# Weighed samples of a deformable convolution: the four corners of a value stored side by side and summed by one reduction

## The chip, the cores and the metric

The kernel runs on one core of a Trainium2 chip. The metric is the device time of one execution, in microseconds. Each TensorE matmul, VectorE operation, ScalarE activation and GpSimd gather below belongs to this one core; the engines run side by side and meet by semaphores.

## The reference

Four blocks follow one another on x of shape (4, 128, 32, 32): an attention with 32 reduced channels (L0), a bottleneck with a deformable convolution (L1), an attention with 16 query channels (L2) and a group norm with an attention of 128 channels (L3). The change lies in L1. What L1 computes:

```python
h = relu(bn(conv1x1(x, w1)))                 # 128 -> 32 channels
off = conv3x3(h, woff) + boff                # 27 channels: 9 taps of (y, x) and a mask
y, x_ = off[:, :18] + base positions         # one sampling place per tap and pixel
mask = sigmoid(off[:, 18:])
samp = (gather(y0, x0) * (wy0 * wx0) + gather(y0, x0 + 1) * (wy0 * wx1)
      + gather(y0 + 1, x0) * (wy1 * wx0) + gather(y0 + 1, x0 + 1) * (wy1 * wx1)) * mask
out = einsum('bckhw,ock->bohw', samp, w2) + b2
return relu(bn(conv1x1(relu(bn(out)), w3)) + x)
```

So each sampled value is a sum over four corners, each a gathered value times a weight: for each pixel 9 taps x 32 channels.

## The kernel before, in words

**Work and tiles.** A batch is one image of 1024 pixels, in 8 tiles of 128 pixels; a pixel is a partition. "(3,7)" is batch 3, tile 7. Everything is fp32 (P = 128, R = 32 channels, TAPS = 9, CORNERS = 4).

**The table.** Per batch the kernel builds a table in DRAM, one row per cell of 2 x 2 neighbouring pixels: 4 corners x 32 channels = 128 floats. `l1_rows` on VectorE (lines 1758 to 1769) works out the row of each tap, `l1_corners` (1774 to 1787) the four weights of each tap; its last four operations, at line 1787, write 72 results each, one corner each, into `corner_w`, where the four corners of a tap lie side by side, so that each of them stores every fourth float. Line 1783 does two products of the same size with results side by side.

**The gather.** GpSimd runs 4 x 8 x 9 = 288 indirect DMAs (line 323), one per batch, tile and tap; each brings one table row per pixel into `got[:, t, k, :]`, 128 floats (corner outermost, channel innermost). `got` has 8 slots, one per tile. Before tile t of the next batch it waits for `slot_free`, which the weighing increments.

**The weighing and the additions.** `l1_weigh` waits for the nine gathers of its tile and for `turn_w`, the 36 weights of the tile, which ScalarE copies into PSUM (line 1171) after its copy of the tile before. It multiplies 1152 gathered floats by their weights into `weighed` (line 1796), in the same layout (tap, corner, channel). `l1_add` adds corners 2 and 3 onto 0 and 1 (line 1807, 576 elements), drains, and adds the two remaining corners into `samples` (line 1809, 288 elements: tap, channel). `samples` has two buffers, freed by TensorE's transposes (`st_mm`).

**Behind it.** TensorE's `l1_turn` (line 488) transposes the samples of a tile, ScalarE copies them (`samplesT`), and when all 8 tiles of a batch are there `l1_conv2` (line 496) and `l1_conv3` (line 511) follow, then `l1_end` on VectorE (line 1819), and with it the batch's L2 and L3.

**The order of work.** Each engine has its instructions in one order written out by hand. L0 of batches 1 to 3, then L2 and L3 of the batches before, are interleaved with the tiles of L1: on VectorE `l1_weigh` and `l1_add` of a tile stand between the row maxima (line 1714 for L0 and L2, line 1897 for L3), the norms (1746, 1838, 1840), the residual additions (1753, 1846, 1914) and so on; on TensorE `l1_turn` stands between scores (360, 391, 625), transposes (635) and values (572, 647). Mostly the next block's operations stand between two tiles of L1. After tile (3,7) come the rest of L1 of batch 3, its L2 and its L3, with nothing gathered any more.

Of the kernel before, what the change touches and what calls it, by code (L numbers as in the profile page):

```python
# [7 lines left out]
P = 128  # L8
# [3 lines left out]
R = 32  # L12
QK2 = C // 8
TAPS = 9
CORNERS = 4
# [37 lines left out]
def build(nc, x_dram, weights_dram, out_dram):  # L53
    fp32, fp32r, bf16, int32 = mybir.dt.float32, mybir.dt.float32r, mybir.dt.bfloat16, mybir.dt.int32
    ALU, ACT, X = mybir.AluOpType, mybir.ActivationFunctionType, mybir.AxisListType.X
# [3 lines left out]
    with ctx:  # L59
        def sb(name, shape, dt=fp32):  # L60
            return ctx.enter_context(nc.sbuf_tensor(name, shape, dt))

        def sem(name):
            return ctx.enter_context(nc.semaphore(name))
# [50 lines left out]
        got = sb("got", [P, TILES, TAPS, CORNERS * R])  # L115
        weighed = sb("weighed", [P, TAPS, CORNERS * R])
        samples = sb("samples", [P, 2, TAPS * R])
# [65 lines left out]
        slot_free = sem("slot_free")  # L183
        sample_ready, st_mm, st_copied = sem("sample_ready"), sem("st_mm"), sem("st_copied")
# [72 lines left out]
        turn_w = d1[:, TURNS * P:TURNS * P + TAPS * CORNERS]  # L257
# [1449 lines left out]
        def _(dve):  # L1707
# [85 lines left out]
            def l1_weigh(b, t):  # L1793
                dve.wait_ge(got_sem[t], 16 * TAPS * (b + 1))
                dve.wait_ge(turn_w_ready, TILES * b + t + 1)
                nc.vector.tensor_tensor(weighed[:, :, :].rearrange("p k (c r) -> p (k c) r", r=R),  # L1796
                                        got[:, t, :, :].rearrange("p k (c r) -> p (k c) r", r=R),
                                        turn_w.rearrange("p (k a) -> p k a", a=1)
                                        .to_broadcast([P, TAPS * CORNERS, R]), ALU.mult).then_inc(slot_free, 1)
                dve.drain()  # L1800
                if t == TILES - 1:
                    dve.sem_inc(table_free, 1)

            def l1_add(b, t):
                if TILES * b + t >= 2:
                    dve.wait_ge(st_mm, TILES * b + t - 1)
                nc.vector.tensor_tensor(weighed[:, :, 0:2 * R], weighed[:, :, 0:2 * R], weighed[:, :, 2 * R:4 * R], ALU.add)
                dve.drain()
                nc.vector.tensor_tensor(samples[:, t % 2, :].rearrange("p (k r) -> p k r", r=R), weighed[:, :, 0:R],
                                        weighed[:, :, R:2 * R], ALU.add).then_inc(sample_ready, 1)  # L1810
                dve.drain()

            def l1_samples(b, t):
                l1_weigh(b, t)
                l1_add(b, t)
# [160 lines left out]
            for n in range(4, 8):  # L1976
                l0_max(2, n)
            shift_parts(1, shift0_ready)
            l1_weigh(0, 0)
            l1_add(0, 0)  # L1980
            l1_weigh(0, 1)
            l1_add(0, 1)
            l0_norm(1, 0)
            l0_q(3, 0)
# [357 lines left out]
```

## Time and profile before

| what | value |
|---|---|
| median of 3 runs | 548.77 us (544.84 to 549.81) |
| the profiled execution, its own time | 544.07 us |
| its span | 542.3 us |
| granted TensorE clock, mean | 0.953 |
| TensorE busy | 485.2 us, 89% |
| VectorE busy | 316.7 us, 58% |
| ScalarE busy | 289.7 us, 53% |
| GpSimd busy | 277.5 us, 51% |

The span is the part of the execution that the trace covers; 1.8 us of the execution's time lie outside it. Shares are averages over the span. TensorE's matmuls are pipelined, so that its busy share is not its share of peak. A row of the trace names an engine, a line of the kernel, and the tiles written and read (`weighed<-got,pd` writes `weighed` from `got` and a PSUM tile); in brackets stands how long the engine was idle before it, and what ended this.

### The profile page before, as it was taken

To read this page: it belongs to the slowest core of one execution; us is meant where nothing else is said; L and a number is where in the kernel's file an instruction comes from. 1 tells how busy PE (TensorE), PEld (TensorE's weight loads), DVE (VectorE), ACT (ScalarE), POOL (GpSimd) and SP (SyncE) were. 2 spreads that over 40 slices of the span, in tenths; PEclk is the share of its full clock that TensorE was granted. 3 is DMA by queue.
4 is the path that set the end of the run, shared out by engine and by line. 5 is a ranking of instruction groups with operands and counts; after the bars stand their busy time and mean duration, and the time that the engine had idled before them with its cause. 6 is when DMAs were issued, how large, how long until landed. Compare 5 with 4: busy or idle time off the path is not lost.

```text
span 542.3 us, 7578 instructions
## 1 busy us (share of the span) xinstructions
PE 485.2 (89%) x2756; PEld 328.3 (61%) x2756; DVE 316.7 (58%) x560; ACT 289.7 (53%) x517; POOL 277.5 (51%) x292
## 2 busy tenths in 40 slices
PE   6897899787889799899988899998989899898997
PEld 4434464434534369557766847685956667594776
DVE  4746454657557676775387675478476567125322
ACT  5366632773576475247565436675525565532553
POOL 0000177777777777777777777777777500000000
PEclk9998759989999689999999999999899999799999
DMA  6000111113122111113113111113111100100001
GB/s 230 0 1 1 49 54 52 52 53 97 50 68 81 51 54 55 48 54 99 54 51 93 51 52 54 53 51 93 54 54 48 45 1 1 39 1 1 1 1 39
DMA packets 12708, 26.94 MB, mean 50 GB/s; under 512 B 4992, under 2 KB 5888, under 8 KB 12672
## 3 DMA queue, kind: packets, MB, share of 16 engines
q0 software_dynamic: 9216, 18.89, 11.7%
q1 hardware_dynamic: 3024, 6.52, 3.2%
q10 hardware_dynamic: 432, 1.05, 0.5%
q8 instruction: 22, 0.36, 0.3%
q14 instruction: 14, 0.11, 0.1%
HBM read 21.99 MB, written 4.46 MB: 49 GB/s over the span
## 4 chain that ended last, share of the span: by engine, by line
POOL 51%; PE 23%; issue 17%; DVE 3%; ACT 3%; DMA 2%; DVEq 1%; POOLq 0%; ACTq 0%
POOL got L323 51%; PE pd L647 4%; PE pq L391 2%; PE pq L635 2%; DVE neg_max L1714 2%; PE pc L416 1%; PE pc L625 1%; PE pa L625 1%; PE pa L572 1%; ACT cells L1221 1%; DMA xall<-x_dram 1%; PE pa L360 1%; PE pc L572 1%; PE pa L340 1%; PE pc L360 1%
## 5 line engine op out<-in xcount | busy, mean ns | idle before, releaser
L323 POOL DMA_INDIRECT got<-cell_table,rows_all x288 | 277.3, 963 | 152.5 <-issue 87.5
L1714 DVE TENSOR_REDUCE neg_max<-pa 128x1 f32<-128x1024 f32 x48 | 58.7, 1223 | 34.8 <-PE pa L360 34.3
L647 PEld LDWEIGHTS pd<-v3T,probsT 128*128 128x128 f32 x512 | 60.5, 192 | 7.0 <-ACT probsT L1171 3.6
L647 PE MATMUL pd<-v3T,probsT 128*128 128x128 f32 x512 | 63.0, 277 | 1.0 <-ACT probsT L1171 0.7
L391 PE MATMUL pq<-q_stack,k_stack 128*128 128x512 f32 x120 | 55.4, 511 | 7.8 <-ACT expT L1205 4.6
L1796 DVE TENSOR_TENSOR weighed<-got,pd 128x1152 f32<-128x1152 f32 x32 | 43.2, 1349 | 24.5 <-ACT pd L1171 15.7
L360 PE MATMUL pa<-k_stack,q_stack 96*128 96x512 f32 x96 | 40.7, 512 | 9.2 <-DVE neg_max L1714 9.2
L1205 ACT ACTIVATE expT<-pq 128x512 f32<-128x512 f32 x64 | 35.6, 595 | 21.9 <-PE pq L391 21.0
L1171 ACT ACTIVATE probsT<-pq 128x1024 f32<-128x1024 f32 (+1 forms) x32 | 32.3, 1008 | 24.8 <-PE pq L635 18.0
L391 PEld LDWEIGHTS pq<-q_stack,k_stack 128*128 128x128 f32 x120 | 24.5, 216 | 31.4 <-ACT expT L1205 14.1
L1309 ACT ACTIVATE expT<-pq 128x512 f32<-128x512 f32 x56 | 31.1, 595 | 12.3 <-PE pq L391 11.6
L635 PEld LDWEIGHTS pq<-wts,probs 128*128 128x128 f32 x256 | 29.2, 141 | 9.2 <-issue 6.0
L360 PEld LDWEIGHTS pa<-k_stack,q_stack 96*128 96x128 f32 x96 | 18.9, 230 | 25.2 <-DVE neg_max L1714 20.2
L416 PE MATMUL pc<-expT,vT 128*64 128x512 f32 x128 | 33.9, 648 | 0.1
L635 PE MATMUL pq<-wts,probs 128*128 128x128 f32 x256 | 33.4, 274 | 0.6 <-ACT probs L1339 0.5
L1171 ACT ACTIVATE samplesT<-pd 96x384 f32<-96x384 f32 x32 | 15.4, 482 | 34.3 <-PE pd L488 34.2
L1221 ACT ACTIVATE cells<-pd,bn_t,bn_s 32x512 f32<-32x512 f32 x32 | 24.6, 770 | 13.5 <-PE pd L449 12.9
L1897 DVE TENSOR_REDUCE neg_max<-pa 128x1 f32<-128x1024 f32 x16 | 19.5, 1222 | 20.8 <-PE pa L625 20.7
L625 PE MATMUL pc<-k,q_offs 128*128 128x512 f32 x64 | 30.3, 596 | 0.0
L625 PE MATMUL pa<-k,q_offs 128*128 128x512 f32 x64 | 30.2, 595 | 0.0
L1897 DVE TENSOR_REDUCE neg_max<-pc 128x1 f32<-128x1024 f32 x16 | 19.5, 1220 | 15.2 <-PE pc L625 15.2
L572 PE MATMUL pa<-vT,expT 128*128 128x129 f32 x192 | 25.7, 291 | 0.9 <-ACT expT L1309 0.9
(180 smaller groups left out, 792.0 us busy)
## 6 DMA issues: line engine op xcount, KB each, us to landing
got<-cell_table,rows_all POOLq DMA_INDIRECT x288, 2.4
cell_table<-tabS SPq DMA_DIRECT2D x4, 512.0 KB, 2.9
out_dram<-cells SPq DMA_DIRECT2D x7, 256.0 KB, 2.1
xall<-x_dram SPq DMA_DIRECT2D x2, 512.0 KB, 8.4
wts<-weights_dram SPq DMA_DIRECT2D x1, 778.5 KB, 5.9
xall<-x_dram ACTq DMA_DIRECT2D x2, 256.0 KB, 5.0
xall<-x_dram ACTq DMA_DIRECT2D x1, 512.0 KB, 8.2
cell_table<-tabS SPq DMA_DIRECT2D x4, 64.0 KB, 2.8
```

The lines of the kernel that those rows point to most:

```text
L323: nc.gpsimd.indirect_dma_start(got[:, t, k, :], None, tables[b % 2], bass.IndirectOffsetOnAxis(ap=rows_all[:, b, at:at + 1], axis=0)).then ...
L360: last = nc.tensor.matmul(pair[:, half(h)], q_stack[stack][0:3 * R, tile(t)], k_stack[stack][0:3 * R, half(h)], start=True, stop=True)
L391: nc.tensor.matmul(bank, k_stack[stack][:, tile(j)], q_stack[stack][:, half(h)], start=True, stop=True)\
L416: last = nc.tensor.matmul(o0_bank(b, h)[2 * R * n:2 * R * (n + 1), :], vT0[:, j, :], expT[:, j, half(h)], start=g == 0, stop=g == TILES // ...
L572: last = nc.tensor.matmul(o2_bank(t), expT[:, j, tile(t)], vT[:, j, :], start=j == 0, stop=j == TILES - 1)
L625: last = nc.tensor.matmul(pair[:, half(h)], q3[:, tile(t)], k3[:, half(h)], start=True, stop=True)
L635: last = nc.tensor.transpose(pq[:, tile(j)], probs[:, t % 2, tile(j)], ident)
L647: last = nc.tensor.matmul(d0[:, 0:C], probsT[:, tile(j)], v3T[:, j, :], start=j == 0, stop=j == TILES - 1)
L1171: return nc.scalar.activation(to, bank, ACT.Copy)
L1714: nc.vector.tensor_reduce(neg_max[:, t:t + 1], pair[:, :], axis=X, op=ALU.max, negate=True)\
L1796: nc.vector.tensor_tensor(weighed[:, :, :].rearrange("p k (c r) -> p (k c) r", r=R), got[:, t, :, :].rearrange("p k (c r) -> p (k c) r", r=R),
L1897: nc.vector.tensor_reduce(neg_max3[:, t:t + 1], (pa, pc)[t % 2][:, :], axis=X, op=ALU.max, negate=True)\
```

## The change

The weighing stores its products in another order: tap, channel, corner, with the corner innermost, so that consecutive results of the instruction (channel by channel) are 4 floats apart. What it reads, and in which order, is as before. The two additions and the drain between them are replaced by one `tensor_reduce` over the innermost 4 floats, which reads 1152 contiguous floats and writes the 288 of `samples`. Waits and semaphores stay where they are.

```diff
 def l1_weigh(b, t):
     dve.wait_ge(got_sem[t], 16 * TAPS * (b + 1))
     dve.wait_ge(turn_w_ready, TILES * b + t + 1)
-    nc.vector.tensor_tensor(weighed[:, :, :].rearrange("p k (c r) -> p (k c) r", r=R),
-                            got[:, t, :, :].rearrange("p k (c r) -> p (k c) r", r=R),
-                            turn_w.rearrange("p (k a) -> p k a", a=1)
-                            .to_broadcast([P, TAPS * CORNERS, R]), ALU.mult).then_inc(slot_free, 1)
+
+    nc.vector.tensor_tensor(weighed[:, :, :].rearrange("p k (r c) -> p k c r", c=CORNERS),
+                            got[:, t, :, :].rearrange("p k (c r) -> p k c r", r=R),
+                            turn_w.rearrange("p (k c a) -> p k c a", c=CORNERS, a=1)
+                            .to_broadcast([P, TAPS, CORNERS, R]), ALU.mult).then_inc(slot_free, 1)
     dve.drain()
...
 def l1_add(b, t):
     if TILES * b + t >= 2:
         dve.wait_ge(st_mm, TILES * b + t - 1)
-    nc.vector.tensor_tensor(weighed[:, :, 0:2 * R], weighed[:, :, 0:2 * R], weighed[:, :, 2 * R:4 * R], ALU.add)
-    dve.drain()
-    nc.vector.tensor_tensor(samples[:, t % 2, :].rearrange("p (k r) -> p k r", r=R), weighed[:, :, 0:R],
-                            weighed[:, :, R:2 * R], ALU.add).then_inc(sample_ready, 1)
+    nc.vector.tensor_reduce(samples[:, t % 2, :], weighed[:, :, :].rearrange("p k (r c) -> p (k r) c", c=CORNERS),
+                            axis=X, op=ALU.add).then_inc(sample_ready, 1)
     dve.drain()
```

## Rows read from the trace of the kernel before

**Rows 1.** The page: TensorE's busy share, the chain by engine, the gathers' group.

```profile
PE 485.2 (89%) x2756; PEld 328.3 (61%) x2756; DVE 316.7 (58%) x560; ACT 289.7 (53%) x517; POOL 277.5 (51%) x292
...
POOL 51%; PE 23%; issue 17%; DVE 3%; ACT 3%; DMA 2%; DVEq 1%; POOLq 0%; ACTq 0%
...
L323 POOL DMA_INDIRECT got<-cell_table,rows_all x288 | 277.3, 963 | 152.5 <-issue 87.5
```

**Rows 2.** The chain in order of time, 425 to 445 us: start, length, what.

```profile
431.79 1.35 DVE weighed L1796
...
433.28 0.76 DVE weighed L1807
...
434.11 0.47 DVE samples L1809
```

**Rows 3.** Busy time (instructions) in two stages of the gathers' part.

```profile
249.60:340.50 90.90, 85.38 (x555) 63.86 (x554) 58.61 (x96) 49.44 (x90) 68.99 (x72) 1.00 0.21 65
340.50:431.80 91.30, 86.33 (x552) 64.77 (x549) 57.27 (x94) 49.99 (x90) 68.45 (x71) 0.98 0.19 58
```

The columns: the stretch, its length, busy us of PE, PEld (weight loads), DVE, ACT and POOL, then granted clock, DMA share and GB/s.

**Rows 4.** Who waited for whom, 65 to 432 us: total us, times, longest.

```profile
DVE weighed L1796 <- DMA got<-cell_table,rows_all: 8.7, 3, 4.7
...
PE pa L360 <- DVE neg_max L1714: 7.1, 7, 1.3
```

**Rows 5.** Timeline at tiles (2,7) and (3,7), VectorE and TensorE.

```profile
340.48 1.35 DVE L1796 TENSOR_TENSOR weighed<-got,pd 128x1152 f32<-128x1152 f32 x1 [3.85 <-DMA got<-cell_table,rows_all]
...
343.31 0.53 PE L488 MATMUL pd<-wts,samples 128*96 128x128 f32 x3 [0.58 <-DVE samples L1809]
...
434.62 0.53 PE L488 MATMUL pd<-wts,samples 128*96 128x128 f32 x3 [2.36 <-DVE samples L1809]
```

**Rows 6.** Timeline: slot 3 weighed in batch 1, its first gather in batch 2.

```profile
218.06 1.34 DVE L1796 TENSOR_TENSOR weighed<-got,pd 128x1152 f32<-128x1152 f32 x1
...
281.84 0.95 POOL L323 DMA_INDIRECT got<-cell_table,rows_all  x1 [0.30 <-issue]
```

**Rows 7.** VectorE's groups by line and shape: busy us, mean ns, idle before.

```profile
L1714 DVE TENSOR_REDUCE neg_max<-pa 128x1 f32<-128x1024 f32 x48 | 58.7, 1223 | 34.8 <-PE pa L360 34.3
...
L1807 DVE TENSOR_TENSOR weighed<-weighed 128x576 f32<-128x576 f32 x32 | 24.2, 757 | 2.7
...
L1809 DVE TENSOR_TENSOR samples<-weighed 128x288 f32<-128x288 f32 x32 | 14.8, 461 | 2.4
L1892 DVE TENSOR_SCALAR q_offs<-pc,bq3s 128x512 f32<-128x512 f32 x8 | 5.9, 751 | 4.1 <-PE pc L608 3.8
...
L1887 DVE TENSOR_SCALAR h<-x,gscale,gbias 128x512 f32<-128x512 f32 x8 | 4.0, 546 | 0.3
```

**Rows 8.** Lines 1787 and 1783: duration ns min/median/max, first and last start.

```profile
L1787 DVE TENSOR_TENSOR corner_w<-wy,probsT x16: 279/290/310, 74.1 to 210.5; 128x72 f32<-128x72 f32 x16
```

```profile
L1783 DVE TENSOR_TENSOR wy<-probsT x8: 219/231/302, 73.7 to 209.8; 128x72 f32<-128x72 f32 x8
```

**Rows 9.** Timeline: the four operations of line 1787 in batch 0, merged.

```profile
74.15 0.72 DVE L1787 TENSOR_TENSOR corner_w<-wy,probsT 128x72 f32<-128x72 f32 x4
```

**Rows 10.** Timeline, 354 to 432 us: TensorE and VectorE behind tiles (3,0) to (3,6).

```profile
359.69 1.41 DVE L1709 SCALAR_TENSOR_TENSOR k_stack<-pa,wts,k_stack 32x512 fp32r<-32x512 f32 x2 [1.25 <-ACT k_stack L1278]
```

```profile
379.33 0.84 PE L488 MATMUL pd<-wts,samples 128*96 128x128 f32 x3
...
398.71 0.66 PE L581 MATMUL pq<-wts,oT 128*128 128x128 f32 x4 [0.72 <-DVE oT L1840]
...
420.97 0.49 PE L488 MATMUL pd<-wts,samples 128*96 128x128 f32 x3
```

**Rows 11.** Timeline, 408 to 411 us: a gather beside the additions of tile (3,4).

```profile
408.46 0.75 DVE L1807 TENSOR_TENSOR weighed<-weighed 128x576 f32<-128x576 f32 x1
408.53 1.50 POOL L323 DMA_INDIRECT got<-cell_table,rows_all  x1 [0.30 <-issue]
...
409.29 0.46 DVE L1809 TENSOR_TENSOR samples<-weighed 128x288 f32<-128x288 f32 x1
```

## The prediction

> **What bounds the kernel now.** The page first: its busy shares, then its chain of waits [rows 1]. TensorE (PE) is busy for 89% of the span, and yet half of the chain that ended last is GpSimd's gathers. Then the chain in order of time around the last gather [rows 2]: up to there nearly every piece is a gather, with 0.30 us of issue between two; at 431.79 the last has landed, and tile (3,7) (batch 3, tile 7) goes through the weighing and both additions to TensorE's transposes and second convolution. From there the chain is TensorE work until 542.3. So the kernel has two parts: up to 431.8 us a stream of 288 gathers sets a floor, and TensorE and VectorE run beside it in an order written by hand; after that TensorE alone counts, and none of the changed code runs.
>
> How tight is each in the first part? The windows by stage [rows 3]: TensorE is busy for 85.4 and 86.3 us of two stages of 91 us, VectorE for 58. TensorE is nearly the bound itself. The waits [rows 4]: the 32 weighings waited for a gather three times only, 8.7 us together, at most 4.7, which is (3,7)'s; 3.85 is (2,7)'s [rows 5]. TensorE's own waits behind these two were 0.58 and 2.36 us [rows 5]. These 2.9 us are all the room that TensorE has before a delay of its stream reaches the end, and also all that it could win if the gathers came sooner.
>
> Could a slower weighing hold up the gathers? A slot is refilled 8 tiles later. The closest case of the 24 is slot 3 of batch 1: weighed from 218.06, filled anew from 281.84 [rows 6], over 62 us later. That cover can't be used up by any price below.
>
> **The change, part by part.**
>
> *The two additions* take 757 and 461 ns [rows 7], and with the 0.07 us between them (from start to start 0.83 [rows 2]) 1.29 us. In their place stands one reduction of 1152 elements to 288 from SBUF, which the trace doesn't show. Nearest rows [rows 7]: the reductions of 1024 elements from PSUM take 1.22 us, 1.19 ns per element, which is 1.37 for 1152; the weighing has 1152 elements and takes 1.35 [rows 2]. From above: if each of the 288 results cost an element's time more (the two additions differ by 288 elements and 296 ns), 0.30 more, 1.65. From below: a one-input operation of 512 elements takes 0.55 us from SBUF and 0.75 from PSUM; if the reduction ran at that better pace, about 1.35 x 0.55/0.75 = 1.0. I take 1.35, the row of its own kind, so +0.06 us a tile (from -0.3 to +0.36).
>
> *The weighing* keeps its operands, its 1152 products and its reading order. Only the store changes: neighbouring results now lie four floats, 16 bytes, apart. The nearest row is the corner weights at line 1787, which store 72 results exactly so, against the products at line 1783, 72 results stored side by side from the same kinds of operands: medians of 290 and 231 ns [rows 8], 59 ns more. A gain is excluded, since the reading is as before. Bounds: nothing, if the 59 ns is a fixed cost or belongs to the operands (+0.06 at most); proportional, 0.82 ns per result, x 1152 = +0.94 us; and one whole element time per result with a little of it hidden in a short instruction, 1152 x 1.03 = +1.19. Against a full price stands that the four at line 1787 follow each other quickly: 0.72 us for all, one alone 0.29, so 0.143 from start to start [rows 9], 2.0 ns per result, which just leaves room for a doubled store and proves none. I take the middle of the two prices, +1.07: the weighing takes about 2.42 us.
>
> The Trainium skill, page "SBUF — State Buffer", in its remark on cachelines (section "Door 1: The DMA port swizzle"), says that SBUF is served in lines of 16 bytes and that an access stream which goes to a new line each time pays a penalty. That speaks against exactly this store, and it agrees with the longer row at line 1787; the page prices no VectorE store, so the sum goes by the rows.
>
> *Sum per tile*: 1.07 + 0.06 = +1.13 us on VectorE, 36 us over 32 tiles, on an engine that is idle for over a third of either stage [rows 3]. What of it reaches TensorE? I followed the seven tiles (3,0) to (3,6) in the timeline, four of whose turning points stand in [rows 10]. (3,0): idle of 0.47 and 1.25 before the next two results that TensorE needs takes it all. (3,1): its samples were ready at 378.79, TensorE took them at 379.33: 0.54 of room, 0.59 passes on. (3,2): idle of 1.04, 1.66 and 2.22 follows: nothing. (3,3): VectorE is busy without a gap until the result that TensorE waits for at 398.71: all 1.13. (3,4): 1.26 idle right behind: nothing. (3,5): ready at 420.66, taken at 420.97: 0.82 passes on. (3,6): ready at 425.75, taken at 427.39: nothing. Together 2.54 of 7.9, a share of 0.32.
>
> The terms: 31 tiles before the last x 1.13 x 0.32 = 11.2 us of delay of TensorE's stream; less the 2.9 us that it waits anyway at (2,7) and (3,7); then the last tile, which lies on the chain with nothing beside it [rows 2]: +1.13. **+9.4 us.** The rest, from 436 on, only moves. The profiled execution took 544.07 us (span 542.3 and 1.8 around it), so 553.5 for its like. The median of the runs shown is 4.7 us above it; carried over, the forecast is 558.2 us.
>
> *What the change gives back.* The gathers of 0.94 us are sometimes longer: their mean is 963 ns [rows 1] against a median of 944, of which by far the most of them are within a few ns, 288 x 19 ns = 5.5 us in all. Of the 25 that took over 0.97 us, 22 overlap one of the two additions, and end just after it; one is shown, 1.50 us long, behind an addition that began just before it [rows 11]. Beside weighings and the reductions for maxima lie many gathers of 0.94.  So the additions, with two inputs in SBUF, hold GpSimd up, and both go. The stream would end some 5.3 us earlier. In my sum that is worth nothing, as TensorE and VectorE arrive later than the last gather anyhow; it counts in the first rival.
>
> The Trainium skill says as much, in the same page's section "Who interferes with whom": an instruction of VectorE with two SBUF inputs is in GpSimd's way when that reads SBUF, one with a single SBUF input isn't. The trace agrees (22 of 25).
>
> **The rivals.**
>
> *A, the store costs nothing.* For it: the pace of the four at line 1787 [rows 9], and the chance that the 59 ns is a fixed cost. Then the tile costs +0.06 and the gathers end 5.3 us earlier. TensorE can use 2.9 of that, since it is ready for (3,7)'s transposes 2.36 us before the samples, and 0.58 more is won at (2,7). The +0.06 of each tile costs 31 x 0.06 x 0.32 = 0.6, and 0.06 once more: -2.9 + 0.7 = -2.2: 541.9, or 546.6 by the median. Faster than before, though less than 1%. The point at which the sign turns: x(31 x 0.32 + 1) = 2.9, x = 0.27 us per tile.
>
> *B, the price is there but mostly covered.* If the earlier tiles pass on a tenth: 3.5 - 2.9 + 1.13 = +1.7, 545.8 or 550.5. For it: VectorE has over a third of its time free [rows 3]. Against: TensorE already waits behind VectorE in this part, for maxima seven times [rows 4].
>
> *C, VectorE becomes the bound in stretches.* With 1.25 us per tile and a share of 0.6: 23.3 - 2.9 + 1.25 = +21.6, 565.7 or 570.4. For it: each existing wait of TensorE behind VectorE, as that for the maxima [rows 4], grows one for one, and most lie in the early batches, where I did not follow the tiles. Against: the seven tiles that I followed.
>
> *D, the reduction runs faster than I think* (1.0 us) and the store costs nothing: then -0.3 a tile and TensorE's waits behind VectorE shrink: -2.9 - 0.3 - 31 x 0.3 x 0.32 = -6.2, 537.9 or 542.6. It needs both unknowns at their low ends.
>
> **How the numbers follow.** About 1%, 5.5 us, is what a measurement of this kernel tells from no change. Forecast 0.52, A 0.20, B 0.12, C 0.11, D 0.05. Slower by over 1%: nine tenths of the forecast's and all of C's, 0.58. Within 1%: the rest of the forecast, B, and most of A, 0.35. Faster by over 1%: D and a little of A, 0.07. Likeliest case alone: with 1.0 to 1.55 us per tile (both prices at their highest) the same sum gives +8.0 to +14.0, 557 to 563. The whole range takes in A below, and most of C above: 544 to 568.
>
> **What the profile after would show.** The weighing at about 2.4 us (A: 1.35; between 2.3 and 2.55 the price is as bounded). One reduction per tile at 1.35. VectorE's busy time up by some 35 us to 352. Gathers without long ones, mean 0.945, last one landing at 426 to 427. No weighing of (3,7) waiting for its gather; the chain before 440 on TensorE and VectorE and no longer on GpSimd. After the last weighing as before, TensorE's 110 us. I am wrong if the weighing stays under 1.6 us, or if it is at 2.4 and the start of (3,7) has moved by less than 3 us.

## The result and the profile after

The changed kernel takes 567.1 us (median of 4 executions, 563.3 to 568.8) against 546.8 before (4 executions, 544.5 to 549.8): a ratio of 1.036, 95% interval 1.027 to 1.044, slower by some 20 us. The direction of the prediction holds. The time lies inside its range, by 0.9 us, and only because the range was drawn wide enough to take in most of rival C; the forecast's own figure, +9.4 us, is half of what came. The ratios below leave out executions that lay well above the fastest of their kernel, most of all two of the four of `reduce_only` and seven of the twelve of `mix_23`.

The profiled execution took 565.97 us, its span is 564.2. The page of the changed kernel, in the order of the page: busy shares, the granted TensorE clock in 40 slices, the chain by engine.

```profile
PE 496.9 (88%) x2756; PEld 333.4 (59%) x2756; DVE 349.3 (62%) x528; ACT 290.2 (51%) x517; POOL 272.3 (48%) x292
...
PEclk9998759789879868999999999999899999889999
...
PE 60%; DVE 21%; DVEq 7%; ACT 7%; issue 3%; DMA 1%; ACTq 0%
```

Three things stand here. VectorE's busy time rose by 32.6 us. The same 2756 matmuls are busy for 11.7 us longer than in [rows 1], at a lower mean clock (0.936 against 0.953), so about half of the 21.9 us by which the span grew is longer matmuls, the other half more idle time. That holds against this one execution of before; a fairer partner comes further down. And GpSimd is gone from the chain that ended last, where it was 51%: the gathers bound nothing any more.

The new instructions by line (duration in ns, least, median, greatest; first and last start in us), then the gathers, all of the changed kernel:

```profile
L1797 DVE TENSOR_TENSOR weighed<-got,pd x32: 2199/2266/2432, 91.2 to 452.9; 128x1152 f32<-128x1152 f32 x32
```

```profile
L1808 DVE TENSOR_REDUCE samples<-weighed x32: 1334/1353/1354, 93.6 to 455.3; 128x288 f32<-128x1152 f32 x32
```

```profile
L323 POOL DMA_INDIRECT got<-cell_table,rows_all x288: 940/945/1079, 67.5 to 426.1; - x144
```

The weighing went from 1.35 to 2.27 us: 0.918 us more for 1152 results, 0.80 ns each. The reduction takes 1.351, as forecast. From the start of the weighing to the end of the samples a tile took 2.738 us (median of 32) and takes 3.725: +0.987. And the gathers lost their long ones: the greatest was 1.5 us [rows 11], now it is 1.08; their last starts 3.3 us earlier, although the first starts 2.0 later.

At tile (3,7), VectorE and TensorE of the changed kernel:

```profile
452.89 2.29 DVE L1797 TENSOR_TENSOR weighed<-got,pd 128x1152 f32<-128x1152 f32 x1 [1.31 <-ACT pd L1171]
```

```profile
456.73 0.53 PE L488 MATMUL pd<-wts,samples 128*96 128x128 f32 x3 [0.18 <-DVE samples L1808]
```

Against [rows 2] and [rows 5]: the weighing starts 21.1 us later, when its gather had long landed, and TensorE's wait of 2.36 us has shrunk to 0.18. From there to the end it is 111.3 us, before 110.5. So all but 0.8 us was lost ahead of this tile.

### The profile page after: what moved, and what is told of

It is laid out like the page before. It is cut to its first block, busy times and chain, and to the rows that moved or that the text cites. A ratio compares the mean times of both kernels' runs of the same rounds, so it can differ in the third digit from the quotient of the medians.

```text
span 564.2 us, 7514 instructions
## 1 busy us (share of the span) xinstructions
PE 496.9 (88%) x2756; PEld 333.4 (59%) x2756; DVE 349.3 (62%) x528; ACT 290.2 (51%) x517; POOL 272.3 (48%) x292
## 4 chain that ended last, share of the span: by engine, by line
PE 60%; DVE 21%; DVEq 7%; ACT 7%; issue 3%; DMA 1%; ACTq 0%
PE pd L647 8%; DVEq L1801 5%; DVE samples L1808 5%; PE pc L416 5%; DVE weighed L1797 5%; DVE neg_max L1714 4%; PE pq L391 4%; PE pa L360 4%; PE pc L625 4%; PE pa L625 4%; PE pa L572 4%; PE pq L635 3%; PE pc L572 3%; PE pd L572 2%; ACT cells L1221 2%
## 5 line engine op out<-in xcount | busy, mean ns | idle before, releaser
L323 POOL DMA_INDIRECT got<-cell_table,rows_all x288 | 272.1, 945 | 154.5 <-issue 87.2
L1797 DVE TENSOR_TENSOR weighed<-got,pd 128x1152 f32<-128x1152 f32 x32 | 72.5, 2267 | 19.1 <-ACT pd L1171 19.1
L360 PE MATMUL pa<-k_stack,q_stack 96*128 96x512 f32 x96 | 41.5, 519 | 10.2 <-DVE neg_max L1714 9.8
L1808 DVE TENSOR_REDUCE samples<-weighed 128x288 f32<-128x1152 f32 x32 | 43.2, 1351 | 2.8
L1309 ACT ACTIVATE expT<-pq 128x512 f32<-128x512 f32 x56 | 30.9, 595 | 14.6 <-PE pq L391 14.1
L416 PE MATMUL pc<-expT,vT 128*64 128x512 f32 x128 | 36.4, 690 | 0.1
```

The source lines that it names most:

```text
L323: nc.gpsimd.indirect_dma_start(got[:, t, k, :], None, tables[b % 2], bass.IndirectOffsetOnAxis(ap=rows_all[:, b, at:at + 1], axis=0)).then ...
L360: last = nc.tensor.matmul(pair[:, half(h)], q_stack[stack][0:3 * R, tile(t)], k_stack[stack][0:3 * R, half(h)], start=True, stop=True)
L416: last = nc.tensor.matmul(o0_bank(b, h)[2 * R * n:2 * R * (n + 1), :], vT0[:, j, :], expT[:, j, half(h)], start=g == 0, stop=g == TILES // ...
L1797: nc.vector.tensor_tensor(weighed[:, :, :].rearrange("p k (r c) -> p k c r", c=CORNERS), got[:, t, :, :].rearrange("p k (c r) -> p k c r", ...
L1808: nc.vector.tensor_reduce(samples[:, t % 2, :], weighed[:, :, :].rearrange("p k (r c) -> p (k r) c", c=CORNERS), axis=X, op=ALU.add).then_ ...
```

## The experiments

**What the stores and reads cost.** Three kernels vary the layout alone.

`reduce_only`: the weighing stores as before, the reduction gathers the corners.

```diff
-weighed[:, :, :].rearrange("p k (r c) -> p (k r) c", c=CORNERS)   # reduce, changed kernel
+weighed[:, :, :].rearrange("p k (c r) -> p k r c", r=R)           # with the weighing of before
```

> The weighing as before, and one reduction of 1152 floats that now reads each value's four corners 32 floats apart. If only spaced stores are dear: weighing 1.35 us, reduction 1.35, gathers 0.945 without long ones, and the time -2 us (rival A of the prediction, 0.5% at most). If spaced reads are dear as well: the reduction at about 2.25 us and +17 to +20 us, as the change.

`read_order`: the weighing stores side by side and reads `got` 32 floats apart. The lines are shortened.

```diff
-nc.vector.tensor_tensor(weighed "p k (r c) -> p k c r", got "p k (c r) -> p k c r", turn_w over [k, c, R])
+nc.vector.tensor_tensor(weighed "p k (r c) -> p k r c", got "p k (c r) -> p k r c", turn_w over [k, R, c])
```

> The weighing stores its products side by side in the changed layout and instead reads the gathered corners 32 floats apart; the reduction as in the change. If spaced reads cost as they did for the reduction (0.81 us for 1152): weighing 2.15 us, and time a little under the changed kernel, +14 to +19 against before. If reading two operands hides it: weighing 1.35 us and time at before or 2 us under it.

`pairs`: the corner is split into y and x, and only x lies innermost, so that neighbouring results are 2 floats apart. Only the two patterns are shown.

```diff
+weighed[:, :, :].rearrange("p k (y r x) -> p (k y) x r", y=2, x=2)   # the store
+weighed[:, :, :].rearrange("p k (y r x) -> p k r y x", y=2, x=2), axis=XY   # the reduction
```

> Spacing halved: the weighing stores two corners side by side (neighbouring results 2 floats apart, two of them in each 16 bytes), one reduction over both remaining axes sums the four. If the price hangs on a new 16-byte line for each result: weighing 1.35 us, reduction 1.35 (or up to 1.8, as it reads two pieces per value), and time at or below before, -2 to +5 us. If any spacing costs: weighing 1.8 us or more and +10 to +20.

Measured, the changed groups by line, of `reduce_only`, `read_order` and `pairs` (two lines) in turn:

```profile
L1807 DVE TENSOR_REDUCE samples<-weighed x32: 2118/2168/2202, 90.9 to 455.0; 128x288 f32<-128x1152 f32 x32
```

```profile
L1797 DVE TENSOR_TENSOR weighed<-got,pd x32: 2141/2183/2250, 90.0 to 455.1; 128x1152 f32<-128x1152 f32 x32
```

```profile
L1797 DVE TENSOR_TENSOR weighed<-got,pd x32: 1333/1352/1391, 89.7 to 436.1; 128x1152 f32<-128x1152 f32 x32
```

```profile
L1808 DVE TENSOR_REDUCE samples<-weighed x32: 1333/1352/1354, 91.1 to 437.6; 128x288 f32<-128x1152 f32 x32
```

Spaced reads cost nearly what spaced stores do: 0.82 us in the reduction, 0.84 in the weighing. (In `read_order` the walk through the weights in PSUM changed as well, so the 0.84 need not all be `got`'s; `reduce_only` has no such second change.) A spacing of 8 bytes costs nothing in the store, one of 16 bytes 0.92. That fits the Trainium skill's remark on cachelines ("SBUF — State Buffer", section "Door 1: The DMA port swizzle"), that two accesses to a 16-byte line are enough for full speed. Spacings of 8 and 16 bytes are all that was tried for stores, 128 for reads, and the reduction of `pairs` reads each value in two pieces of 8 bytes, 256 bytes apart, without loss. The times, as ratios to before with the 95% interval: `read_order` 1.0275 (1.0188 to 1.0363), 15 us, as its first expectation had it. `reduce_only` 1.0236 (1.0165 to 1.0306), 13 us: its reduction as the second expectation said, its time less than the +17 to +20, though the median of all four executions is 17 us over before. `pairs` 0.9985 (0.9938 to 1.0032), no difference that can be told.

`pairs` is also rival A put to the test: a tile costs 0.067 us more than before, and GpSimd is not held up (its last gather starts at 424.6, 4.8 us earlier than before). I had put this at -2.2 us; 0.9985 is -0.8, with zero inside its interval. Ending the gathers sooner is worth nothing that can be measured here.

**Is it VectorE's time, or the store itself?** Fillers are reductions on VectorE that read constants and whose result nobody uses.

```diff
 def l1_weigh(b, t):
     ...
     dve.drain()
+    nc.vector.tensor_reduce(pad[:, :], wts[:, 0:729], axis=X, op=ALU.max)   # pad_all: every batch, on the kernel before
```

> The kernel before, with one VectorE reduction of 729 constant floats (about 0.91 us, 0.98 with its gap, what the change added per tile) behind each of the 32 weighings; stores and additions as before. Theory T, only VectorE's time counts: the same loss as the change, +18 to +21 us. Rival S, the spaced store does something more than take time (it disturbs another engine or the clock): clearly less, about +9 by the forecast's share of 0.32.

It gave 1.0255 (1.0191 to 1.0318), 14 us, between the two. `pairs_pad` was to match the changed kernel's tile without a store spaced by 16 bytes (670 floats, on `pairs`).

> The pairs kernel with a filler on VectorE of 670 constant floats (about 0.85 us and its gap, 0.92 together) behind each weighing, so that a tile takes what it takes in the changed kernel without any store to a new 16-byte line per result. If the spaced store costs VectorE's time and nothing else: the changed kernel's time, +18 to +21 us. If it also disturbs others: 3 us or more below it.

1.0244 (1.0201 to 1.0287), 13.3 us, which by its expectation spoke for a disturbance. But its trace showed the tile at 3.56 us, and `pad_all`'s likewise, against 3.73 of the changed kernel: the gaps around the filler were smaller than I had reckoned, and in both kernels a tile was 0.82 us longer than before instead of 0.99. So the filler was made longer.

```diff
-    nc.vector.tensor_reduce(pad[:, :], wts[:, 0:670], axis=X, op=ALU.max)
+    nc.vector.tensor_reduce(pad[:, :], wts[:, 0:828], axis=X, op=ALU.max)
```

> The pairs kernel with a longer filler, 828 constant floats. In the trace of pairs_pad a tile took 3.56 us from the start of its weighing to the end of its reduction, in the changed kernel 3.72; 158 floats more make up the 0.165. If the spaced store costs VectorE's time and nothing else, the time is the changed kernel's: +18 to +20 us (ratio 1.033 to 1.037). If 13.4 us for 0.82 us a tile scales only in proportion, +16 at most (1.029), and the rest of the changed kernel's loss is from something else in the spaced store.

VectorE's groups of `pad_exact` (mean ns, idle before); its tile measured 3.721 us:

```profile
L1798 DVE TENSOR_TENSOR weighed<-got,pd 128x1152 f32<-128x1152 f32 x32 | 43.2, 1351 | 17.5 <-ACT pd L1172 17.5
L1810 DVE TENSOR_REDUCE samples<-weighed 128x288 f32<-128x1152 f32 x32 | 43.0, 1343 | 0.0
...
L1803 DVE TENSOR_REDUCE pad<-wts 128x1 f32<-128x828 f32 x32 | 32.5, 1016 | 3.0
```

1.0369 (1.0323 to 1.0415), 20 us: the changed kernel's loss, with no store in the weighing spaced by more than 8 bytes. The spaced store costs VectorE's time; no second cost is needed. The last 0.165 us per tile, 5.3 us over 32, cost about 6.8 us; the two intervals lie apart, so that it costs something is clear, but that it costs more than the 5.3 is not shown. By what a tile takes longer than before: 0.07 us nothing, 0.82 some 13 to 14 us, 0.88 (`reduce_only`) 13, 0.91 (`read_order`) 15, 0.99 some 18 to 20.

**Where is it lost?** Starts of the weighings, less those of the kernel before (from the traces, in us; the last two rows are explained below):

| kernel | (0,7) | (1,7) | (2,7) | (3,6) | (3,7) |
|---|---|---|---|---|---|
| changed | 10.2 | 17.4 | 21.8 | 23.5 | 21.1 |
| pairs | 9.6 | 9.2 | 9.3 | 7.5 | 4.3 |
| mix_01 | 8.5 | 14.9 | 16.3 | 14.6 | 11.4 |
| mix_23 | -0.4 | -0.6 | 3.6 | 4.3 | 1.8 |

The changed kernel's row looks like a loss of nearly a full microsecond per tile in batches 0 and 1, half of one in batch 2 and a quarter in batch 3. So I took the early batches to be where it happens, and ran fillers in halves.

```diff
+    if b in (0, 1):        # pad_23: (2, 3)
+        nc.vector.tensor_reduce(pad[:, :], wts[:, 0:729], axis=X, op=ALU.max)
```

> The same filler for batches 0 and 1 only (16 tiles). If the share passed on is near 1 in the early batches and lower later, as the starts of the weighings suggest: 15 us of delay at (1,7), less up to 2.9 us of waits later, +12. If the share is even over the batches: 16 x 0.98 x 0.32 - 2.9 = +2.

> The same filler for batches 2 and 3 only. If the early batches pass on most: batch 2 gives 4 us, batch 3 gives 2, less 2.9 of waits, plus the last tile's 1.0: +4. If the share is even: +3 by the forecast, +12 if it is even at the 0.7 that the whole change showed.

1.0175 (1.0075 to 1.0276) and 1.0165 (1.007 to 1.026), 9.6 and 9.0 us: each lies between its own expectations, and no difference between the halves can be told. As both intervals were wide, the same was done with the change itself (`l1_weigh_spaced` is the changed kernel's weighing, `l1_weigh_pairs` that of `pairs`).

```diff
+def l1_weigh(b, t):
+    (l1_weigh_spaced if b in (0, 1) else l1_weigh_pairs)(b, t)   # mix_23: (2, 3); l1_add likewise
```

> The changed weighing and reduction (3.62 us a tile) in batches 0 and 1, those of the pairs kernel (2.70 us) in batches 2 and 3. By the starts of the weighings in the fillers' traces the early batches pass on nearly all: 17 to 20 us of delay at (1,7), some of it taken up later by waits: +12 to +15 us against before. Rival, even share over the batches: half of the change's loss, +10.

> The reverse: changed in batches 2 and 3, pairs in 0 and 1. By the traces: 4 us of delay each or less, 2.9 taken up at the last tile, +1.0 for that tile itself: +2 to +5 us. Rival, even share: +10.

1.0174 (1.0131 to 1.0217) and 1.0126 (1.008 to 1.0173). The first is +9.5 us, less than the +12 to +15 that I expected of it; the second is +6.9 and above its +2 to +5. The even share came nearer.

What had misled me stands in the table's row of `pairs`: at (0,7) it is 9.6 us behind, with a tile only 0.067 us longer than before. Between TensorE's transposes of (0,0) and those of (1,0) it runs the same 356 matmuls in both; before, this stretch takes 83.0 us, 68.9 of them busy; in `pairs` it is 9.1 us longer, with 10.3 us more of busy time and 1.2 less of idle time. Matmuls that take longer, and no wait, make it late there. The granted clock fits. The windows of 130 to 150 us, before (first), then `pairs` (columns as in [rows 3]):

```profile
130.00:140.00 10.00, 9.41 (x66) 6.11 (x65) 6.79 (x10) 3.76 (x10) 7.56 (x9) 1.00 0.35 104
140.00:150.00 10.00, 7.71 (x38) 4.39 (x38) 6.12 (x18) 6.85 (x13) 7.84 (x8) 1.00 0.18 54
```

```profile
130.00:140.00 10.00, 9.15 (x30) 5.90 (x30) 5.24 (x7) 1.91 (x5) 7.56 (x9) 0.54 0.35 112
140.00:150.00 10.00, 9.44 (x51) 5.57 (x51) 4.54 (x7) 3.42 (x8) 7.56 (x9) 0.77 0.20 55
```

At 0.54 TensorE is for nearly all of the stretch at the lower of its two levels, 1.2 GHz, and gets through 30 matmuls in 9.15 busy us where before it got through 66 (in part others, as the stream is late) in 9.41. This comes and goes from execution to execution of one kernel, as two profiles of the changed kernel show (the first one, then `after_again`, which is the same kernel run once more):

```profile
130.00:140.00 10.00, 6.24 (x38) 3.99 (x34) 7.12 (x9) 1.92 (x5) 7.56 (x8) 1.00 0.34 111
```

```profile
130.00:140.00 10.00, 9.33 (x30) 6.08 (x30) 5.04 (x7) 1.91 (x5) 7.56 (x9) 0.50 0.36 112
```

Yet these two took 565.97 and 565.28 us and start (0,7) 10.2 and 9.9 us late: the first has its low stretches elsewhere (0.66 from 100 to 110 us, 0.70 from 160 to 170). So this one stretch doesn't decide the time.

The times of single executions fall into groups by the mean clock. Beside `mix_01` the kernel before took 543.8 to 546.3 us at mean clocks of 0.946 to 0.962, 548.8 to 549.1 at 0.934 to 0.938, and 546.9 to 548.2 between. The profile of before, on which I predicted, is of the first kind (0.953). The changed kernel's 8 executions are all of the second (0.931 to 0.939). Against executions of before at such a clock, some 549 to 551 us, its 563 to 569 are a loss of about 16 us; by this grouping the other 3 to 4 us are there because before is often of the better kind. The grouping goes by the mean clock, which longer waits may lower too, so the split is an estimate. `pairs` bears it out in its page:

```profile
PE 492.9 (90%) x2756; PEld 331.1 (61%) x2756; DVE 320.3 (59%) x528; ACT 289.6 (53%) x517; POOL 272.6 (50%) x292
```

Its profile has the changed kernel's clock (0.938 against 0.936) and a span of 546.7 us. Against it the changed kernel's span is 17.5 us longer, of which TensorE is busy for 4.0 and idle for 13.5. So at an equal clock most of the loss is TensorE waiting, and not the half that the comparison with [rows 1] gave.

`mix_23` ran in both kinds: 546.7 to 548.5 at 0.959 and 0.962, 552.9 and 554.2 at 0.947 and 0.944, and seven times 556.1 to 559.7 at 0.933 to 0.942. The median of all twelve is 556.2, 9.9 us over before, and that of `mix_01` 556.8, 10.6 over. So in the usual execution of these two the halves cost the same within what can be told; only in one with a good clock is the late half as cheap as I had read from the traces, and `mix_23`'s profile (0.962) is such a one.

**Is the clock a cause?** Both timelines show TensorE waiting behind the weighing of tile (0,1), in the kernel before and in the changed one (timeline, TensorE):

```profile
98.55 0.44 PE L437 MATMUL pc<-wts,probs 128*128 128x128 f32 x2 [1.64 <-DVE probs L1746]
```

```profile
101.51 0.69 PE L437 MATMUL pc<-wts,probs 128*128 128x128 f32 x2 [2.59 <-DVE probs L1746]
```

The wait grew by 0.95 us, and the two transposes behind it take 0.69 instead of 0.44: the clock has fallen. `after_fill` gives TensorE something to do in this wait; `after_again` is the changed kernel, run beside it.

```diff
+def fill(count):
+    pe.wait_ge(off_read, 1)
+    for _ in range(count):
+        nc.tensor.matmul(d0, ident16[:, :], ident16[:, None, :].to_broadcast([P, 4, P]), start=True, stop=True)
...
+fill(11)
 l0_turn(1, 0)
```

> The changed kernel once more, on the chip and in the rounds of the next three, as their base. +19 to +21 us against before, weighing 2.27 us, reduction 1.35.

> The changed kernel, with 11 idle matmuls of 512 columns (about 0.21 us each) that TensorE runs at 99 us, in the 2.59 us in which it waits behind the weighing and reduction of tile (0,1). Theory K, part of the loss comes from TensorE's clock, which falls behind these longer waits: the granted clock of 100 to 110 us goes from 0.66 back to about 1.0, and 3 us or more of the loss go with it. Rival W, only the waits themselves cost: nothing is gained, 0 to +1 us against the changed kernel.

The windows of 90 to 120 us, `after_again` first, then `after_fill`:

```profile
90.00:100.00 10.00, 6.85 (x43) 5.14 (x42) 6.60 (x7) 5.21 (x11) 7.56 (x9) 0.90 0.18 53
100.00:110.00 10.00, 8.74 (x31) 4.46 (x31) 4.18 (x7) 6.16 (x13) 7.56 (x9) 0.76 0.21 55
110.00:120.00 10.00, 7.63 (x25) 3.20 (x23) 6.70 (x9) 6.44 (x11) 7.56 (x9) 0.92 0.19 52
```

```profile
90.00:100.00 10.00, 9.77 (x58) 5.64 (x54) 7.68 (x7) 5.22 (x11) 7.56 (x9) 1.00 0.18 52
100.00:110.00 10.00, 7.70 (x36) 4.35 (x35) 5.44 (x11) 6.74 (x14) 7.57 (x9) 1.00 0.21 55
110.00:120.00 10.00, 7.54 (x21) 3.12 (x20) 6.28 (x8) 5.84 (x10) 7.56 (x9) 0.81 0.18 52
...
130.00:140.00 10.00, 8.74 (x27) 5.50 (x27) 5.04 (x7) 1.92 (x5) 7.56 (x9) 0.50 0.36 111
```

The clock from 90 to 110 us came back to 1.00, so the wait is what lets it fall there. The time did not: 1.0328 (1.024 to 1.0416) against 1.0337 (1.027 to 1.0405) for `after_again`. From 110 to 120 us the clock is lower than without the filler, 0.81 against 0.92, and from 130 us it is low in both. One stretch mended gives nothing that can be measured, as rival W of the expectation had it; that waits alone cost follows only for this stretch. How much of the 20 us would go if the clock never fell in batches 0 and 1 was not tried and stays open, and so does what tips an execution into the one kind or the other.

## Why the prediction was right or wrong

*The price of the store.* Right in kind, a little high: +0.92 us instead of +1.07, and the weighing at 2.27 us just under the 2.3 to 2.55 that was named. The proportional price from line 1787 (0.82 ns per result, [rows 8]) was the true one (0.80); the middle that I took between it and a whole element time was a hedge that only cost accuracy.

*The reduction.* 1.351 us, as the row of its own kind had it; a tile +0.987 instead of +1.13.

*The port.* Right. (Of the gathers over 0.97 us in the trace of before I count 26, 23 of them beside an addition, one more of each than the prediction has.) The trace of after has no long gather; `pad_all`, which keeps the additions, still has them up to 1.5 us:

```profile
L324 POOL DMA_INDIRECT got<-cell_table,rows_all x288: 942/947/1497, 65.7 to 430.9; - x144
```

That the gain is worthless while TensorE's stream is later than the last gather held, and even `pairs` turned 4.8 us of it into nothing measurable.

*What of it reaches TensorE: the step that failed.* "Together 2.54 of 7.9, a share of 0.32", taken for 31 tiles. For the tiles that I followed it was, if anything, high: from the start of (3,0) to that of (3,6) the changed kernel lost 0.7 us for 5.9 added, and from that of (2,7) 1.8 for 6.9, a share of 0.26. Over all, 19 to 20 us less the 1.0 of the last tile and plus the 2.9 of room is 21 to 22 of 30.6 us, a share of 0.7. A part of that is the clock: against the profile of `pairs`, at an equal clock, 17.5 us less 0.9 of the last tile is 16.6 of the 28.5 that 31 tiles add, a share of 0.58. Against the profile of before, batch 2 passed on 4.3 us of 7.9 and batch 1 7.2. I had written that most of TensorE's waits behind VectorE lie in the early batches, and still carried the share of the calmest stage over to them. That the sign came out right needed only a price well above the 0.27 us at which it turns; that the time fell into the range was the width of the range.

*The room of 2.9 us.* Against the profile of before it was there: in every row of the table the delay shrinks from (3,6) to (3,7), by 2.4 to 3.2 us, and `mix_23`'s profile has the span that this gives (544.9, +2.6; 3.6 + 0.7 - 2.5 + 1.0 makes +2.8). But `pairs`, which costs a tile next to nothing, has used it up as well, being 9 us late from batch 0 on by longer matmuls alone. An execution of before at that clock presumably does the same, and then a change finds no room left; no trace of one is at hand, so this is argued.

*The clock.* Not in the sum at all. 3 to 4 us, by the groups above, and a part of the waits' price that these runs don't separate.

*The rivals.* A was excluded by the weighing's 2.27 us. B (mostly covered) fits the late batches alone, in `mix_23`'s executions with a good clock; no kernel with the full price in all batches came near its +1.7 us (`pad_exact`'s best, at a clock of 0.945, is 559.4). C had the larger share (0.6 against 0.58 to 0.7), a price too high, and the early batches as its place: its account is nearer to what happened than the forecast's, its +21.6 us too. But VectorE as a bound in stretches was not shown, only that added time passes on.

## What to carry to other kernels

Before an engine's added time is called covered, follow some of its instances in every stage and not in one: cover found where another engine runs steadily need not hold in a stage where that engine already waits. One profile is one execution: look at the clock of the other executions too, since the room that one of them shows may be gone in others, most of all in those of the changed kernel. And where two instructions are fused at the price of an access spaced by 16 bytes, try half the spacing first: here a store every 8 bytes cost nothing and one every 16 bytes 0.9 us a tile. (Even so the fusion alone gained nothing that can be told: `pairs`, 0.9985.)

## What the runs showed of the hardware that I had not expected

A VectorE store of fp32 results 8 bytes apart is as fast as a dense one (1.351 us for 1152), one 16 bytes apart takes 2.267. Reads 128 bytes apart cost about the same surcharge, 0.82 us for 1152 elements in a reduction and 0.84 in a product. The price is 0.71 to 0.80 ns per element, where an element takes some 1.03 ([rows 7], the two additions); at 72 elements it is 0.82 [rows 8]. And a kernel whose executions agree within 1% can still fall into groups: some 545 us with a mean granted clock of 0.95, some 549 with 0.935, and a few between. The one trace of the second kind at almost unchanged cost (`pairs`) has granted clocks of 0.54 and 0.77 from 130 to 150 us, so TensorE is at 1.2 GHz for some 14 of these 20 us, where the trace of the first kind has it at 2.4 GHz throughout.
